# x of the later batches loaded with features on partitions, its token factors turned into rows

## The reference

```python
def _layernorm(x, axis=-1, eps=1e-05):
    m = jnp.mean(x, axis=axis, keepdims=True)
    v = jnp.var(x, axis=axis, keepdims=True)
    return (x - m) / jnp.sqrt(v + eps)
...
        q = (x @ Wq.T).reshape(b, s, H, HD).transpose(0, 2, 1, 3)
        k = (x @ Wk.T).reshape(b, s, HKV, HD).transpose(0, 2, 1, 3)
        v = (x @ Wv.T).reshape(b, s, HKV, HD).transpose(0, 2, 1, 3)
        q = _rmsnorm(q, q_norm_w)
        k = _rmsnorm(k, k_norm_w)
        qg = q.reshape(b, HKV, G, s, HD)
        scores = jnp.einsum('bkgqd,bksd->bkgqs', qg, k) / math.sqrt(HD)
...
        attn = jax.nn.softmax(scores + bias[None], axis=-1)
        out = jnp.einsum('bkgqs,bksd->bkgqd', attn, v)
        out = out.reshape(b, H, s, HD).transpose(0, 2, 1, 3).reshape(b, s, H * HD)
        return out @ Wo.T
...
    x = L0_attn_x
    xn = _layernorm(x, axis=-1)
    s = _L0_attn_ref(xn, ...)
    g = _silu(_L0_ffn_ref(xn, ...))
    x = x + s * g
```

## Time and profile before

| | |
|---|---|
| median of 3 runs (us) | 2654.52 (2654.34 to 2654.75) |
| profiled execution, its time (us) | 2655.72 |
| its span (us) | 2653.9 |
| TensorE busy, clock granted | 2583.1 us, 97%; 0.995 of full |
| VectorE, ScalarE, GpSimd busy | 64%, 66%, 65% |
| DMA | 414.78 MB, mean 156 GB/s; about 0.8 busy to 610 us, then 0.35 to 0.5 |

### The profile page before, as it was taken

The page is one execution under the profiler, slowest core; times in us unless marked ns, Lnnn a source line. Parts: engine busy times, 40 slices in busy tenths (PEclk is TensorE's granted clock), DMA queues, the critical chain, the costliest instruction groups (busy, mean ns, idle before and its releaser), DMA issues.

```text
span 2653.9 us, 39893 instructions
## 1 busy us (share of the span) xinstructions
PE 2583.1 (97%) x13840; PEld 2288.9 (86%) x13840; DVE 1699.8 (64%) x3533; ACT 1764.6 (66%) x4633; POOL 1718.0 (65%) x839
## 2 busy tenths in 40 slices
PE   6789999999999999999999999999999999999997
PEld 5778888888888888888888888888888888888886
DVE  7565656666766665666667666666666756656656
ACT  4565666767767666667766667666777666667764
POOL 3577887785767565655667756565666766656555
PEclk9899999999999999999999999999999999999999
DMA  7868878875354333433344433433334533333323
GB/s 283 289 219 278 265 261 272 271 258 166 118 171 154 113 106 118 140 112 118 106 137 155 128 119 111 144 106 118 109 104 137 189 106 108 115 116 112 112 78 131
DMA packets 171896, 414.78 MB, mean 156 GB/s; under 512 B 31024, under 2 KB 63920, under 8 KB 170800
## 3 DMA queue, kind: packets, MB, share of 16 engines
q1 hardware_dynamic: 170144, 410.19, 47.1%
q10 hardware_dynamic: 1552, 2.04, 0.2%
HBM read 339.81 MB, written 89.13 MB: 162 GB/s over the span
## 4 chain that ended last, share of the span: by engine, by line
PE 90%; DVE 3%; DMA 2%; POOL 2%; ACT 1%; SPq 1%; issue 0%; ACTq 0%; POOLq 0%; DVEq 0%
PE proj L508 21%; PE proj L510 21%; PE proj L509 21%; PE tr L608 5%; PE tr L588 3%; PE sc L508 3%; PE sc L509 3%; PE sc L510 3%; PE ot L509 3%; PE ot L510 3%; PE ot L508 3%; DMA wu<-xtok 1%; PE tr L581 1%; DMA wl<-wu 1%; POOL wl L1081 1%
## 5 line engine op out<-in xcount | busy, mean ns | idle before, releaser
L1081 POOL TENSOR_TENSOR wl<-wl,wh 128x896 fp32r<-128x896 f32 x428 | 909.1, 2156 | 552.3 <-ACT wh L788 552.2
L508 PE MATMUL proj<-wh,xh 128*128 128x448 f32 x1792 | 670.7, 374 | 7.3 <-ACT raw L827 2.2
L509 PE MATMUL proj<-wl,xh 128*128 128x448 f32 x1792 | 657.9, 367 | 0.0
L510 PE MATMUL proj<-wh,xl 128*128 128x448 f32 x1792 | 657.8, 367 | 0.0
L1092 POOL TENSOR_TENSOR wb_lo<-wb_lo,wb_hi 128x1024 fp32r<-128x1024 f32 x128 | 307.7, 2404 | 303.7 <-ACT wb_hi L822 303.7
L879 ACT ACTIVATE misc<-misc,negmax 128x128 f32<-128x128 f32 (+3 forms) x512 | 286.7, 565 | 266.3 <-DVE negmax L1319 266.1
L508 PE MATMUL proj<-o_hi,wb_hi 128*128 128x512 f32 x1024 | 425.2, 415 | 7.4 <-DVE acc L1344 3.5
L1344 DVE TENSOR_TENSOR acc<-acc,proj 128x512 f32<-128x512 f32 x476 | 324.8, 683 | 149.7 <-PE proj L510 147.8
L858 ACT ACTIVATE pT_hi<-tr 128x512 fp32r<-128x512 f32 (+3 forms) x512 | 197.5, 440 | 325.9 <-PE tr L608 325.9
L510 PE MATMUL proj<-o_hi,wb_lo 128*128 128x512 f32 x1024 | 403.6, 394 | 0.0
L509 PE MATMUL proj<-o_lo,wb_hi 128*128 128x512 f32 x1024 | 401.3, 392 | 0.0
(11 more groups left out here) (135 smaller groups left out, 4438.1 us busy)
## 6 DMA issues: line engine op xcount, KB each, us to landing
wl<-wu SPq DMA_DIRECT2D x426, 448.0 KB, 3.9
wb_lo<-wo_in SPq DMA_DIRECT2D x128, 512.0 KB, 3.3
wu<-xtok SPq DMA_DIRECT2D x13, 1792.0 KB, 9.7
wo_in<-wo SPq DMA_DIRECT2D x32, 512.0 KB, 6.2
xtok<-wa SPq DMA_DIRECT2D x52, 256.0 KB, 4.0
wu<-xtok SPq DMA_DIRECT2D x13, 896.0 KB, 6.2
gate_dram<-misc SPq DMA_DIRECT2D x32, 256.0 KB, 5.0
xtok<-xT SPq DMA_DIRECT2D x28, 256.0 KB, 5.1
```

Source lines behind the costliest of these rows:

```text
L508: pe.matmul(out, hi_l, hi_r, start=first, stop=False, skip_group_check=onto)
L509: pe.matmul(out, hi_l, lo_r, start=False, stop=False, skip_group_check=onto)
L510: return pe.matmul(out, lo_l, hi_r, start=False, stop=last, skip_group_check=onto)
L1081: pool.tensor_tensor(w_slot(wl, w), w_slot(wl, w, True), w_slot(wh, w), ALU.subtract).then_inc(w_ready, 1)
```

## The change

For batches 1 to 3, `xtok` is loaded from `xT`, with features on partitions, as 8 chunks of 512 tokens. Nothing of it is turned. The statistics come from single token tiles: `load_rows` brings 128 tokens at a time into the new buffer `rows` in steps (5,0) to (5,3), and `row_stats` reads each. In (6,0) the factors of the tokens, one column per token tile, are copied out to 128 columns each (`spread_rows`). In (6,1) TensorE turns these eight tiles (`turn_tokens`), and VectorE takes the two banks, which now hold the scale and the shift of every token along the row, the same in all partitions. VectorE multiplies the four parts of x by the scale row (`x_mul`, in (6,1)), GpSimd adds the shift row (`x_add`, two in (6,1), two in (6,2)). The high part is then one ScalarE copy of 1024 columns per product (`x_hi_later`), the low part one VectorE subtraction of 1024 columns from `xtok` in SBUF (`x_lo_later`). To make room for `rows`, the bias has one buffer instead of two, and the squares' scratch is two rows instead of six.

```diff
 def x_fills(n, j):
...
-    at = {(6, 3): range(0, 4), (7, 0): range(4, 10), (7, 1): range(10, 14)}
-    return [("x", b + 1, f) for f in at.get((g, j), ())]
+    return [(b + 1, p) for p in {(6, 3): (P1, P2), (7, 0): (P4,), (7, 2): (P5, P3)}.get((g, j), ())]
+def x_late(n, j):
+    b, g = divmod(n, HKV)
+    p = {(6, 3): P7, (7, 0): P6}.get((g, j))
+    return None if p is None or b + 1 == BATCH else (b + 1, p)
...
+            if (n % HKV, j) == (6, 1) and n + HKV < NG:
+                keys += [("r", n // HKV + 1, i) for i in range(2)]
...
-                sp.dma_start(xtok[:], x_tok[b - 1]).then_inc(x_in, 16)
+                chunks = xT[b * NK:b * NK + NK].rearrange("k p n -> p k n")
+                sp.dma_start(flat(xtok).rearrange("p (k n) -> p k n", k=NK), chunks).then_inc(x_in, 16)
+            def load_rows(b, t):
+                if t > 0:
+                    sp.wait_ge(row_stat, NT * (b - 1) + t)
+                elif b > 1:
+                    sp.wait_ge(x_norm, 4 * (b - 1))
+                sp.dma_start(rows, x_tok[b - 1][:, t, :]).then_inc(rows_in, 16)
...
+            def turn_tokens(b, i):
+                key = ("r", b, i)
+                pe.wait_ge(row_spread, b)
+                bank = turn_bank(key)
+                for t in range(NT):
+                    at = i * S + t * P
+                    mm = pe.transpose(bank[:, t * P:t * P + P], rows[:, at:at + P], ident_sb[:])
+                mm.then_inc(tr_done, 1)
...
+                if (n % HKV, j) == (6, 1) and n + HKV < NG:
+                    for i in range(2):
+                        turn_tokens(n // HKV + 1, i)
-                for u in pieces:
+                for u in unit_pieces(n, j):
                     piece(*u)
-                    if fills:
-                        turn_x(fills.pop(0))
...
-            def squares(heads, row, turn):
-                need(act, sq_done, turn - 1)
+            def squares(heads, row, count):
                 for i, head in enumerate(heads):
                     at = (("q0", "q1", "k", "q2", "q3").index(head)) * 4 + row
...
+                    need(act, sq_done, count + i - 1)
+                    act.activation(junk[:, (count + i) % 2, :], raw[:, row, COL[head]:COL[head] + HD],
+                                   ACT.Square, accum_out=ss[:, at:at + 1]).then_inc(sq_done, 1)
...
+            def x_hi_later(b, p):
+                if p in FILL_SUM:
+                    act.wait_ge(sum_ready, 4 * b + FILL_SUM[p])
+                else:
+                    act.wait_ge(x_norm, 4 * (b - 1) + {P1: 1, P2: 2, P4: 4}[p])
+                act.wait_ge(u_done, u_count(HKV * b - 1, p, 1))
+                act.activation(xh[:, p], x_block(p), ACT.Copy).then_inc(x_hi_done, 1)
...
                 elif j != 2:
                     split_product(*[(n + 1, P7), (n + 1, P5), None, (n + 2, P2)][j])
+                if x_late(n, j):
+                    x_hi_later(*x_late(n, j))
...
-                if m >= 2:
-                    wait_alone(pool, scored, 4 * m - 4)
-                pool.tensor_scalar(bias_sb[:, m % 2, :], rel_sb[:], slope[:, m % H:m % H + 1], None,
+                if m >= 1:
+                    wait_alone(pool, scored, 4 * m)
+                pool.tensor_scalar(bias_sb[:], rel_sb[:], slope[:, m % H:m % H + 1], None,
...
+            def x_add(b, i):
+                part, at = x_part(i)
+                pool.wait_ge(x_mul_done, 4 * (b - 1) + i + 1)
+                pool.wait_ge(row_free, 2 * b)
+                shift = rows[:, S + at.start:S + at.stop].unsqueeze(1).to_broadcast([P, 4, 256])
+                pool.tensor_tensor(part, part, shift, ALU.add).then_inc(x_norm, 1)
...
+                if (g, j) == (6, 2) and next_x is not None:
+                    x_add(next_x, 2)
+                    x_add(next_x, 3)
+                if (g, j) == (6, 3) and next_x is not None:
                     x_sum(next_x, P7)
...
+                if (g, j) == (6, 1) and next_x is not None:
+                    x_add(next_x, 0)
+                    x_add(next_x, 1)
+                if (g, j) == (7, 1) and next_x is not None:
+                    x_sum(next_x, P5)
+                    x_sum(next_x, P3)
...
+            def spread_rows(b):
+                dve.wait_ge(ln_newton, 5 * (b + 1))
+                for i, column in enumerate((rinv_x, shift_x)):
+                    place = rows[:, i * S:i * S + S].rearrange("p (t n) -> p t n", t=NT)
+                    ins = dve.tensor_copy(place, column[:].unsqueeze(2).to_broadcast([P, NT, P]))
+                ins.then_inc(row_spread, 1)
+            def take_rows(b, i):
+                dve.wait_ge(tr_done, TR["r", b, i] + 1)
+                dve.tensor_copy(rows[:, i * S:i * S + S], tr_ps[TR["r", b, i] % 3][:]).then_inc(row_free, 1)
+            def x_mul(b, i):
+                part, at = x_part(i)
+                dve.wait_ge(x_in, 16 * b)
+                dve.wait_ge(row_free, 2 * b - 1)
+                factor = rows[:, at].unsqueeze(1).to_broadcast([P, 4, 256])
+                dve.tensor_tensor(part, part, factor, ALU.mult).then_inc(x_mul_done, 1)
+            def x_lo_later(b, p):
+                dve.wait_ge(x_hi_done, x_count(b, p))
+                dve.tensor_tensor(xl[:, p], x_block(p), xh[:, p], ALU.subtract).then_inc(x_ready, 1)
...
-                if j == 2 and g == ln_group(b + 1) and next_x:
+                if (g, j) == (6, 0) and next_x:
                     ln_factors(b + 1)
+                    spread_rows(b + 1)
                 add_out(v, 1)
...
                 add_out(v, 3)
+                if x_late(n, j):
+                    x_lo_later(*x_late(n, j))
```

More of the change, by code:

```diff
@@ L1027, in step @@
                         rsqrt(n + 1, 1)
[L1028 to L1032 removed]
+                if (g, j) == (6, 0) and b + 1 < BATCH:
+                    ln_rsqrt(b + 1)
                 for k in range(3):
                     probs_hi(m, k)
[L1035 to L1039 removed]
                 if m == 0:
@@ L1244, in ln_stats, with row_stats, ln_variance @@
                 ins.then_inc(ln_stat, 1)
-                wait_alone(dve, ln_stat, 2 * b + 1)
+                wait_alone(dve, ln_stat, 1)
+                ln_variance(0)
+            def row_stats(b, t):
+                dve.wait_ge(rows_in, 16 * (NT * (b - 1) + t + 1))
+                for i in range(2):
+                    ins = dve.bn_stats(bn[:, t, 6 * i:6 * i + 6], rows[:, 512 * i:512 * i + 512])
+                ins.then_inc(row_stat, 1)
+                if t == NT - 1:
+                    wait_alone(dve, row_stat, NT * b)
+                    ln_variance(b)
+            def ln_variance(b):
                 for t in range(NT):
@@ L1507, in step @@
                     queries_lo(n, 3)
+                if (g, j) == (6, 1) and next_x:
+                    for i in range(2):
+                        take_rows(b + 1, i)
                 if j == 3 and more:
@@ L1528, in step @@
                     if turned:
-                        x_lo(turned.pop(0))
+                        x_lo_later(*turned.pop(0))
                     if fills:
@@ L1533, in step @@
                         gate_sum(n)
[L1534 to L1535 removed]
+                    if (g, j) == (6, 1) and next_x:
+                        x_mul(b + 1, i)
                     if j == 1 and ending:
```

149 lines of the change are left out of this document (72 added, 77 removed).

## The result

The changed kernel takes 2723.06 us, median of 4 runs (2716.16 to 2732.36), beside 2654.64 us (2654.34 to 2656.37) of the kernel before on the same chip: ratio 1.0259, 95% interval 1.0227 to 1.0290. It is slower, as forecast, but by 68 us instead of 27; the forecast of 2681 us and its range (to 2702) missed.

A forecast was written before the change was run, and what follows sets the result against it. TensorE, busy 97% of the span, was taken to bound the kernel. Its saved work and idle (-25.4 us) and new waits (17.4 us per batch, 52.2 in all) gave +26.8 us on 2654.5, so 2681 us; range 2655 to 2702.

The forecast's parts named there:

- turns and old idle gone, factors turned: TensorE: 168 transposes of x go (25.3 us), 24 factor transposes come (3.4), 3.5 us idle goes; -25.4 us together.
- A: (6,1): TensorE waits for the second bank of factors until VectorE takes query 2's low part; 2.0 us per batch (1.5 to 2.5).
- B: (6,0): making the factors delays VectorE's first pT_lo, which TensorE awaits; 1.2 us per batch (0.5 to 2.5).
- C: (6,2): VectorE's row factors fall within GpSimd's two x_add operations and run late; 1.0 us per batch (0 to 2.5).
- D: (6,3): x_lo of P1 and P2 between VectorE's pieces delays the last piece's take; 2.0 us per batch (0 to 2.8).
- E: Ends of (6,3) and (7,0): x_lo of P7 and P6 delays the next maxima; 6.6 us per batch (5.2 to 9.4).
- F: (7,2): sums and halves of P5 and P3 delay the first pT_lo; 4.6 us per batch (3.3 to 6.5).
- Rival 3: Each small VectorE operation loses to GpSimd in turn in (6,2), (6,3) and (7,2): 2700 to 2708 us; chance 0.08.
- Costed at nothing: Single-tile statistics in group 5, x_mul in (6,1), the one bias buffer, the squares' waits and the loads: no cost assumed.
- Rival 1: Faster: VectorE catches up, hiding the waits of (6,3), (7,0) and (7,2); 2642 us; chance 0.14.
- Rival 2: Mechanism right, but VectorE hardly ever meets GpSimd: 2661 us; chance 0.14.
- Rival 4: The squares' waits act in every group: the forecast and 6 us, 2687 us; chance 0.08.

The follow-up runs named there:

- x5: Kernel before, with three of the four turns in each filler of x left out for batches 1 to 3 (126 of 168); 2642.85 us.
- e1: Changed kernel with VectorE's low halves of P7 and P6 moved behind the next step's fourth score maximum; 2704.06 us.
- e3: Changed kernel with the second bank of token factors turned, and taken by VectorE, behind the first projection piece in (6,1); 2720.37 us.
- e2: Changed kernel with GpSimd's sums of P5 and P3 moved in (7,1) ahead of the low products, behind low_b; 2711.47 us.
- c4_adds_only: Changed kernel with only GpSimd's shift additions moved: P1's in (6,1), the other three in (6,3), none in (6,2); 2710.47 us.
- x3: Kernel before, with a spare long VectorE reciprocal (1408 columns) at the end of four steps of the last batch; 2697.86 us.
- x4: Kernel before, with a spare short VectorE reciprocal (384 columns) at the end of sixteen steps of the last batch; 2703.46 us.
- c1_same: Changed kernel, unedited, run again for a second profile; 2723.92 us.
- e8: Changed kernel with much x work re-placed in groups 6 and 7, GpSimd's additions out of (6,2), ScalarE spreading the factors; 2648.10 us, ratio 0.9977.
- x1: Kernel before, with spare GpSimd additions, both inputs in SBUF, in the last batch; 2668.51 us.
- x2: Kernel before, with spare one-input GpSimd multiplications by a factor per partition in the last batch; 2665.23 us.

## Why the prediction was wrong

The direction and the kind of loss were right, the size not. By its steps, against the first profile:

| step | forecast, us | measured, us |
|---|---|---|
| turns and old idle gone, factors turned | -25.4 | -22.6 |
| A, three batches | 6.0 | 6.2 |
| B | 3.6 | 2.1 |
| C | 3.0 | 6.6 (up to 19 in other executions) |
| D | 6.0 | 4.9 |
| E | 19.8 | 17.5 |
| F | 13.8 | 26.2 |
| group 5 of batch 0 | 0 | 3.1 |
| granted clock | 0 | 12 to 13 |
| not placed | | 5 |
| sum | 26.8 | 61.6 |

- **Base.** The halves of the kernel before hold 24.9 us for x, not 28.8. x5 prices a turn at 0.09 to 0.10 us, not 0.150, so the 168 turns were worth 15 to 16.5 us and not 25.3. The idle rows of these halves sum to 3.9 us (3.5 forecast). The 4.5 to 6 us that remain had no term, and they hid part of the error. The 24 turns of factors at that price are 2.3.
- **A, B, D and E** came within 0.8 us a batch each, and e1 and e3 show that A and E are waits of their place.
- **F failed**: 8.7 us a batch against 4.6, range 3.3 to 6.5. Up to the second low half of x the timeline of the forecast holds: its GpSimd row stands 9.3 us later in the trace after, the sums begin at 730.38 (forecast 721.1) and the first low half ends at 736.2 (727.1). The step that fails is "the row factors (0.9)", with "one more meeting is likely". They took 6.4 us, since all three of them, 12 columns each, meet a GpSimd operation. The sums delay GpSimd, and bias, low_b and low products then follow in one row without gaps. Rival 3, held at 0.08, is what happened here. e2 takes the backlog away and two of the three are free.
- **C** has a second wait, the scaling of keys and queries. I had that operation at 3.00 us in the earlier trace rows and asked only what it does to the row factors. Its size is a matter of luck in each execution, which c4_adds_only takes out: 13.5 us in the median.
- **The clock** had no term at all. x3 and x4 show that it belongs to the price of a wait. The 5 us stretches behind TensorE's waits, taken at one minus their clock, give 12.6 us in the first profile (some 19 in c1_same, counted over its low stretches less TensorE's idle time in them), such as the second of these two:

```profile
740.00:745.00 5.00, 0.00 (x0) 0.00 (x0) 4.90 (x5) 0.00 (x0) 4.22 (x3) 0.69 0.00 2
745.00:750.00 5.00, 4.38 (x17) 3.67 (x18) 3.43 (x11) 0.65 (x3) 0.00 (x0) 0.63 0.09 15
```

- **Costed at nothing.** GpSimd's bias waits for VectorE's maxima, 115.0 us in all, but half a batch without x lasts as long as before (315.3 to 315.4 us), so TensorE pays nothing for it there; the squares take 300 ns as before. In group 5 of batch 0 TensorE waits 3.1 us; whether the statistics do that wasn't tried, and batches 1 and 2 have nothing there.
- **Rivals 1, 2 and 4** did not happen. Rival 1's thought is not wrong in itself: e8 is the change with its steps where VectorE does catch up.
- **Not placed** are 5 us that the rows of waits and clock don't cover. e8 has 5 us of the same kind (18.7 by steps, against 11.4 of waits and 2.3 of turns). Most of it is a part of each wait that its idle row doesn't show. Matmuls overlap: without a wait two of these start 0.46 us apart with one between them, and here, around a wait of 1.27 us in e8, 1.99 us:

```profile
1293.48 0.39 PE L544 MATMUL proj<-o_hi,wb_lo 128*128 128x512 f32 x1
1295.14 0.50 PE L542 MATMUL proj<-o_hi,wb_hi 128*128 128x512 f32 x1 [1.27 <-DVE raw L1428]
1295.47 0.40 PE L543 MATMUL proj<-o_lo,wb_hi 128*128 128x512 f32 x1
```

  Compared in this way at full clock, a wait costs 0.2 to 0.3 us more than its idle row, 3.7 us for the 15 rows of e8. The changed kernel's 27 listed waits, at that price, are some 6 to 7 us, about what is missing.

Beside C, F, x1 and x2: the Trainium skill (SBUF — State Buffer, section SBUF: two separate sides) makes the shared port pair a lock held for a whole instruction; the one that comes second "fully blocks". Rows of this case agree: 12 columns take 2.33 us. It also says that VectorE with two SBUF inputs is shut out by any GpSimd operation that reads SBUF. Here the measurement differs: inside one-input operations, which read SBUF, two-input operations of VectorE kept their times, the row factors of x2 (0.17 us) and the low half at 736.73 (1.21 us).

## What to carry to other kernels

Work moved off a full engine has to be placed, not only counted: nearly the same operations on x cost 86 us or more in one order and 19 in another (e8 also has ScalarE spread the factors). Before a two-input SBUF operation is given to GpSimd, look for the row of such operations that it closes up, and price every VectorE operation with two SBUF inputs that falls into it at a whole GpSimd operation, the short ones too. Add to every predicted stall of TensorE what it costs beyond itself, mostly the clock that follows it: by these runs 0.3 to 0.5 us for each us of stall.
